# Router products of finished tiles: from one run of 98 at the end to one in each step of the group stage

## The reference: what is computed

```python
xn = _layernorm(x)
x = x + gnn(xn, weight, edge_weight, src, dst) + mix(xn[None], ...)[0]
x = x + ffn(_layernorm(x)[None], ...)[0]

# gnn: support = xn @ weight; msgs = edge_weight[:, None] * support[dst]; segment_sum(msgs, src)
# ffn: weights = x @ wr + br                  (the router: one number per node)
#      idx = the KEEP = 6249 nodes with the largest weights
#      y = (gelu(x[idx] @ w1 + b1) @ w2 + b2) * weights[idx]
#      returns x, with y added to the chosen rows
```

## Time and profile before

| | us |
|---|---|
| median of 3 timed runs (3671.89 to 3687.26) | 3671.97 |
| the profiled execution's own time | 3643.18 |
| its span | 3641.4 |
| group stage: first to last add of POOL | 2276.7 to 3133.0 |
| tail: end of the adds to first product of the FFN | about 3134 to 3260 |
| FFN | about 3260 to 3641 |

### The profile page before, as it was taken

One profiled execution on the slowest core, in us unless ns is written; L12 is line 12 of the kernel. 1 busy time (PEld: TensorE's weight loads), 2 busy tenths in 40 slices (PEclk: granted clock), 3 DMA queues, 4 the chain that ended last, 5 costly groups with the idle time before them and its releaser, 6 DMA issues.

```text
span 3641.4 us, 82338 instructions
## 1 busy us (share of the span) xinstructions
PE 3008.8 (83%) x18718; PEld 2284.4 (63%) x18718; DVE 2457.8 (67%) x6616; ACT 1620.0 (44%) x4142; POOL 2036.7 (56%) x2303
## 2 busy tenths in 40 slices
PE   3777757989999778878888885999999999349998
PEld 2444425666666666666666664777777777238887
DVE  7888894444444577677767773999999999862111
ACT  4444413555555444444444443444444444662332
POOL 1444443555555556655656665777777777313433
PEclk7889978999999899899999997999999999759999
DMA  5777735888888777766776776888888888651111
GB/s 169 249 249 249 261 122 188 277 269 276 277 272 274 252 230 228 230 226 225 238 226 223 228 234 219 273 279 276 277 276 276 278 274 275 231 185 52 53 53 43
DMA packets 427483, 818.34 MB, mean 225 GB/s; under 512 B 45499, under 2 KB 203191, under 8 KB 427256
## 3 DMA queue, kind: packets, MB, share of 16 engines
q1 hardware_dynamic: 348376, 559.80, 50.4%
q0 software_dynamic: 78880, 256.49, 18.6%
HBM read 459.96 MB, written 356.17 MB: 224 GB/s over the span
## 4 chain that ended last, share of the span: by engine, by line
PE 43%; POOL 15%; issue 12%; DVE 12%; ACT 6%; POOLq 4%; another core or an unknown queue 3%; DMA 3%; SPq 2%; DVEq 0%; ACTq 0%
POOL acc L738 15%; PE ps L958 15%; PE ps L1145 5%; PE ps L1135 5%; PE ps L971 5%; PE ps L967 2%; POOLq L735 2%; DVE acc L1513 2%; PE ps L1005 2%; ACT rowbuf L1271 2%; PE ps L1014 1%; DMA acc<-bucket_rows 1%; PE ps L929 1%; PE ps L979 1%
## 5 line engine op out<-in xcount | busy, mean ns | idle before, releaser
L706 POOL DMA_INDIRECT sorted_rows<-rowbuf,posu x896 | 925.6, 1033 | 766.4 <-ACT rowbuf L1271 506.9
L958 PE MATMUL ps<-mainbuf 128*128 128x256 bf16 x5376 | 740.3, 283 | 168.1 <-ACT rowbuf L1271 106.1
L1092 PE MATMUL ps<-rowbuf,mainbuf 128*128 128x256 f32 x3584 | 845.7, 393 | 24.2 <-DVE mainbuf L1890 19.4
L1271 ACT ACTIVATE rowbuf<-ps 128x512 f32<-128x512 f32 x896 | 514.6, 593 | 769.6 <-PE ps L958 408.1
L1890 DVE TENSOR_SCALAR mainbuf<-cols,rowbuf 128x128 f32<-128x128 f32 x1792 | 819.2, 526 | 43.6 <-DMA rowbuf<-sorted_rows 34.7
L738 POOL TENSOR_TENSOR acc<-acc,node 128x256 f32 x896 | 673.8, 752 | 196.1 <-POOL acc L738 130.2
L1092 PEld LDWEIGHTS ps<-rowbuf,mainbuf 128*128 128x128 f32 x3584 | 620.0, 189 | 249.8 <-DVE mainbuf L1890 179.6
L958 PEld LDWEIGHTS ps<-mainbuf 128*128 128x128 bf16 x5376 | 510.7, 101 | 305.3 <-ACT rowbuf L1271 154.9
L1365 ACT ACTIVATE node<-ps 128x512 f32<-128x512 f32 x448 | 267.5, 597 | 493.4 <-PE ps L1092 405.0
L1707 DVE TENSOR_SCALAR mainbuf<-mainbuf,lane 128x1024 bf16<-128x1024 bf16 (+1 forms) x256 | 116.4, 455 | 269.1 <-PE ps L958 206.2
L1340 ACT ACTIVATE rowbuf<-ps,fb_c 128x256 f32<-128x256 f32 x200 | 94.8, 474 | 254.1 <-PE ps L1135 252.5
(11 more groups left out here) (354 smaller groups left out, 4702.5 us busy)
## 6 DMA issues: line engine op xcount, KB each, us to landing
rowbuf<-sorted_rows SPq DMA_DIRECT2D x448, 516.0 KB, 4.5
mainbuf<-slot_rows_in_window SPq DMA_DIRECT2D x128, 448.0 KB
acc<-bucket_rows SPq DMA_DIRECT2D x128, 416.0 KB, 6.1
sorted_rows<-node SPq DMA_DIRECT2D x105, 258.0 KB, 2.4
mainbuf<-support_rows SPq DMA_DIRECT2D x128, 192.0 KB
sorted_rows<-rowbuf,posu POOLq DMA_INDIRECT x896
node<-in_x SPq DMA_DIRECT2D x104, 128.0 KB, 5.1
sorted_rows<-rowbuf SPq DMA_DIRECT2D x14, 903.0 KB, 4.9
```

The costliest lines, as they stand in the source:

```text
L706: g.indirect_dma_start(pairs_d, bass.IndirectOffsetOnAxis(posu[:, PC * k + c:PC * k + c + 1], 0), rowbuf[:, S * k + 2 * c:S * k + 2 * c + ...
L958: last = mm(ps[:, MSG + (k + c) % 2, u * C:(u + 1) * C], oht[:, s * P:(s + 1) * P], win[:, k, v * C:(v + 1) * C], start=v == 0, stop=v == 2)
L1092: last = mm(ps[:, GRP + k, h * C:(h + 1) * C], ohw[:, k % 2, s * P:(s + 1) * P], rowbuf[:, BT * k + s, 0:C], start=t == 0, stop=t == 1)
L1271: A(rowbuf[:, S * k + 2 * c:S * k + 2 * c + 2, 0:C], ps[:, MSG + (k + c) % 2, :].rearrange("p (t c) -> p t c", t=2), ACT.Copy).then_inc(ro ...
```

## The change

- DVE gets a `router_product(i)` in each step of the group stage, ahead of the one-hots of pair k = 2: a register load of the tile's number from `turn_row`, a wait for the statistics of the turn before (`stat_done`), and one `tensor_tensor` multiply of the tile's 128 x 256 with `wr` into `dump_v`. For the turns behind the loop it does the same in a loop of its own.
- ACT gets a fourth stat in each turn, k = 3: it waits for `prod_ready` and sums `dump_v` with a Copy with accumulated output into `wts`. The counts of `stat_done` go from three to four a turn.
- The 98 `tensor_tensor_reduce` of DVE behind the statistics are gone.
- The wait for the load of `wr` (`w2_in`) moves from behind the loop into it.

```diff
-        TREAD0, FO0, STAT0 = 2, 2, 3
+        TREAD0, FO0, STAT0 = 2, 2, 4
...
-                act.wait_ge(stat_done, 3 * i + STAT0 + k)
+                act.wait_ge(stat_done, 4 * i + STAT0 + k)
...
+                if k == 3:
+                    act.wait_ge(prod_ready, i + 1)
+                    A(dump_a, dump_v[:, 0, :], ACT.Copy, accum_out=wts[:, ds(c, 1)]).then_inc(stat_done, 1)
...
                     if k > 0:
                         stat(i, c, k - 1)
+                stat(i, c, 3)
...
-                for k in range(3):
+                for k in range(4):
                     stat(i, c, k)
...
+            def router_product(i):
+
+                c = dve.value_load(turn_row[0:1, ds(i, 1)], min_val=0, max_val=NT - 1)
+                dve.wait_ge(stat_done, 4 * i + STAT0)
+                v.tensor_tensor(dump_v[:, 0, :], acc[:, ds(c * C, C)], vec2[:, WR, :], ALU.mult).then_inc(prod_ready, 1)
+
             with dve.Fori(0, steps) as i:
                 for k in range(KB):
+                    if k == 2:
+                        dve.wait_ge(w2_in, 32)
+                        dve.wait_ge(acc_done, RG * i + 1)
+                        router_product(i)
...
-            dve.wait_ge(w2_in, 32)
             turns = dve.value_load(tki[0:1, 6:7], min_val=2, max_val=NTURN)
-            dve.wait_ge(stat_done, 3 * turns + STAT0)
+            with dve.Fori(steps, turns) as i:
+                router_product(i)
+            dve.wait_ge(stat_done, 4 * turns + STAT0)
...
-            for t in range(NT):
-                if t % 4 == 0:
-                    chain.wait()
-                chain.inc(v.tensor_tensor_reduce(dump_v[:, t % 4, :], acc[:, t * C:(t + 1) * C], vec2[:, WR, :], 1.0, 0.0,
-                                                 ALU.mult, ALU.add, wts[:, t:t + 1]))
-            chain.wait()
```

More of the change, by code:

```diff
@@ L325, in gps_layer_kernel @@
             "rows_ready", "norm_set", "xid_ready", "idu_ready", "fo_out", "fo_free"))
-        stat_done = sem("stat_done")
+        stat_done, prod_ready = sem("stat_done"), sem("prod_ready")
         x3_out = [sem(f"x3_out{s}") for s in range(2)]
```

## The result

The changed kernel takes 3687.26 us (median of 20 runs, 3676.17 to 3699.11), the kernel before 3677.60 us (median of 20 runs on the same chip). The ratio is **1.0032, 95% interval 1.0021 to 1.0043**, which is 11.8 us with bounds of 7.7 and 15.8 us. The change costs a little, clear of the noise, and less than the 0.5% that the prediction took as the limit for "no change". The forecast was +21.9 us.

A forecast was written before the change was run, and what follows sets the result against it. POOL's adds, 7.65 us a step, were taken as the bound. 14.0 + 14.0 - 6.1 = +21.9 us on the profiled 3643.18 gave 3665; with the 28.8 us to the runs' median carried over, 3694 us, range 3665 to 3725.

The forecast's parts named there:

- within 0.5%: Whole kernel: outcome that the time changes by less than about 0.5%, 18.4 us; chance 0.42.
- POOL's adds set the pace, DVE has 17 places and 16 one-hots: Group stage: adds run 7.65 us a step; DVE gets through only in gaps between them, with one place to spare.
- The product as second in a gap, +14.0 us: Group stage: a product second in a gap between adds delays the add by 0.125 us, over 112 steps.
- Half of the landing waits become lost places, +14.0 us: Group stage: with all places taken, half of DVE's 0.25 us a step of row waits is paid, 0.125 us times 112.
- Costed at nothing: Group stage: register load, ACT's fourth stat and the product's wait for `stat_done` are taken as covered, at no cost.
- The tail, -6.1 us: After the loop: removing 98 products saves 7.4 us until the stores hold the fetch, less 1.3 us for later ACT lots.
- hidden: Group stage rival: products use the spare place and the pace stays; -6 to +8 us, chance 0.22.
- all of the tail: Tail rival: all 37 us come off if stores do not hold the fetch; -35.6 us, 3636, chance 0.03.
- The add waits for the whole product: Group stage rival: the add begins when the product has ended, 0.25 us a step; +36 us, 3708, chance 0.10.
- Two places: Group stage rival: product stays first in its gap, leaving 15 places for 16 one-hots; +51 us, 3723, chance 0.20.
- a whole period: Group stage rival: the product costs DVE an add's turn, 0.93 us each step; +98 us, 3770, chance 0.04.
- The signs to look for: Changed profile: steps of 7.77 to 8.0 us, self-paced adds, one add over 0.8 us; wrong if POOL waits over 0.44 us.

The follow-up runs named there:

- e1: Kernel before plus the product in each group-stage step, no fourth stat, tail products kept; ratio 1.0040, stage 872.2 us against 856.3.
- e6: Changed kernel with each product made twice, the second behind a wait for the first; ratio 1.0147 to the kernel before, stage 918.5 us.
- e4: Changed kernel with `wr` copied once to PSUM, so the product reads one SBUF input; ratio 1.0024 to the kernel before, stage 873.0 us.
- e5: Changed kernel with the product over 128 of 256 columns; ratio 1.0009 to the kernel before, stage 865.6 us.
- e8: Changed kernel with `wr` in PSUM and register load, waits and product behind pair 2's first one-hot; ratio 1.0111 to the kernel before, stage 904.2 us.
- e10: Changed kernel with `wr` in PSUM and only the product behind pair 2's first one-hot, load and waits left ahead; ratio 1.0017 to the kernel before, stage 866.3 us.
- e2: Kernel before plus a fourth ACT stat into a scratch column, no group-stage product, tail unchanged; ratio 1.0004, stage 856.4 us.
- e11: Changed kernel with ACT's fourth stat right behind the second and squared deviations last; ratio 1.0026 to the kernel before, stage 873.6 us.
- e3: Kernel before without the 98 router products, nodes chosen by other numbers; ratio 0.9976, stage 856.3 us, fetch 112.0 us after the last add.
- e7: Changed kernel with group-stage loads fetching only the first half of each pair's rows; ratio 0.9994 to the kernel before, stage 865.2 us.
- e7b: Kernel before with group-stage loads fetching only the first half of each pair's rows; ratio 1.0010, stage 862.0 us.
- e9: Kernel before with 12 of the 98 tail products moved ahead of DVE's wait for the last statistics; ratio 0.9993, stage 855.7 us.

## Why the prediction was right, and where its sizes were off

**The result** lies in the range (3665 to 3725) and in "within 0.5%", which had a chance of 0.42 against 0.55 for slower. So the side called more likely did not come. The likeliest value, 3694, lies 7 us above the measured 3687.26. The predicted net cost, +21.9 us, was 10 us above the measured +11.8; the kernel before came out at 3677.60 us and not at 3671.97, and that hides 5.6 us of the miss. Both terms of the stage were too high, by 3 and by 6 us.

- **POOL's adds set the pace, DVE has 17 places and 16 one-hots:** held. (Of the 196 waits for ACT not all can be turns of the loop, as 820 us hold 107; the others are the ordinary 0.17 us. That POOL is never starved stands: one gap at a turn was over 0.5 us before.) One product uses up the rest, at 15.9 us (e1); a second one costs 43.0 (e6).
- **The product as second in a gap, +14.0 us:** the mechanism was right in outline. It measured 0.101 us a step, 11.2 us. The product does come second, but in the long gap of the loop's turn, where it is over before the add; the third, a one-hot, stretches it (e4, e5). The working took the 0.09 us that a product is longer as a delay of the add ahead of which it stands. What was 0.08 to 0.09 us later was the one-hot behind it, so that the size came out near for a neighbouring reason, in part by luck.
- **Half of the landing waits become lost places, +14.0 us:** right in kind, too large. The mean step lies 0.086 us above the median, before it was 0.016: 7.8 us more in 111 steps, which are the long steps. Their cause is shown twice, by the late first one-hot in each and by half loads, where all but one are gone; the late copy of pair 0 makes each a little longer. Of 0.25 us a step of landing waits, 0.07 were paid. The rest didn't arise, since a DVE that is later finds its rows: its waits for rows fell from 34.7 to 10.3 us.
- **Costed at nothing:** the register load, the product's wait and the fourth stat. The load's cover was real: without it, e8 lost 37.9 us to e10, 0.34 us a step, where 0.26 were named. The product never stood for `stat_done`. The fourth stat is 0 where there is slack (e2), and some 2 us where there isn't (e1, e11). "POOL needs only later" held for the copy of pair 0 before the change; with the slack gone, POOL waited for it at 32 turns.
- **The tail, -6.1 us:** measured -6.06, and each of its dates as predicted: the lots 1.29 us later (1.3), `spots` with the ninth lot, the numbers some 16 us ahead of the stores, the stores last. That 37 us of DVE's work were worth only 7.4 is shown by e3 (7.35).
- **The rivals:** "hidden" falls by the median step, and "all of the tail" by e3. "The add waits for the whole product" is wrong: in an ordinary step the product ends before the add starts, and in e7, where it comes second in a gap of 0.17 us as the prediction had it, the add starts while it runs and takes 0.83 us, 0.08 over the usual 0.75. "Two places" and "a whole period" ask for a product that comes first in its gap; it did so once in the changed kernel (945 ns). In e5 the shorter product did so in 105 of 114 turns, at the loop's long gap, and a step still took 7.73 us: coming first did not cost a second place there.
- **The signs to look for:** steps at 7.77 to 8.0 us was met by the mean (7.83) and not by the two groups of steps that make it up, 7.73 and 8.04. That the adds wait for nothing but themselves holds for 78 of 111 steps. The long add was there: 70 of 112 adds at the turn take over 0.8 us, before it was 4. A sign of being wrong was there too, POOL waiting for ACT with more than 0.44 us at the turn, in 32 steps; it was to tell of "two places", and tells of the fourth stat instead, as e1 and e11 don't have it.

What stays open: the greater slack of e5, why the adds of e7b are slower, and the part of the 3.2 us between e1 and the changed kernel that the turn doesn't hold. Not tried: e10 together with e11's order, and a product with two SBUF inputs at e10's place.

## What to carry to other kernels

Where two engines take turns, count places and not busy time, and ask of a new instruction which place it gets and what then stands third. An engine with no place to spare pays for a late transfer, of 0.1 us too, with a lost place, here 0.3 us of the step, and a mean hides this: look at the distances step by step. Before costing work that is removed, look for the wait that comes next; here it left 7.4 of 37 us. And work on an engine that is 44% busy can still make a copy late that the pacing engine waits for, once the slack between them is gone.

## What the runs showed of the hardware

- A VectorE product of 128 x 256 with one operand in PSUM runs wholly beside a GpSimd add of two SBUF inputs: 0.41 us and 0.742 us, both as if alone (e10). With two SBUF inputs it stands until the add's end, 0.82 us for 0.28 us of work (e5).
- A register load with its waits on VectorE, behind a single one-hot, leaves the engine idle for up to 0.7 us ahead of the next instruction, 25.4 us in 48 times (e8). Behind four one-hots nothing of it is seen: the products of the changed kernel have 0.1 us of idle time before them, in sum.
- A VectorE one-hot that ends 0.25 us into a GpSimd add stretches it to 0.82 us, from 0.74 where it ends 0.15 us into it (e10) and 0.72 where it ends 0.12 us into it (changed kernel). Such an add ahead of the loop's turn shortens the gap behind it: 0.83 + 0.37 us in e7, 0.75 + 0.44 before.
- GpSimd's adds take 0.758 us on average in e7b and 0.752 in e9. In e7b the one-hots of 2330 to 2940 us wait for PE and never for rows; that this is the cause is not shown.
